# Adaptive-norm transformer block on one core: values in four sets a stage, a third slot of exponentials, and second halves' queries rotated by GpSimd

## The reference

```python
q = _rmsnorm(x @ wq_a.T, q_a_ln_w) @ wq_b.T           # per head 64 plain + 64 rotary columns
q_pe = _apply_rope(_deinterleave(q_pe), cos, sin)
scores = einsum('bqhd,bkhd->bhqk', q_full, k_full) * softmax_scale
scores = where(causal, scores, finfo.min)
attn = softmax(scores, axis=-1)
out = einsum('bhqk,bkhd->bqhd', attn, v)
out = out.reshape(B, S, H * VD) @ wo.T
```

## Time and profile before

| | us |
|---|---|
| median of 3 runs (721.63 to 721.87) | 721.75 |
| profiled execution, its own time | 721.88 |
| its span | 720.1 |
| TensorE busy | 694.4 (96%) |
| VectorE busy | 523.9 (73%) |
| ScalarE busy | 289.6 (40%) |
| GpSimd busy | 230.3 (32%) |

### The profile page before, as it was taken

The page is one execution under the profiler, slowest core; times in us unless marked ns, Lnnn a source line. Parts: engine busy times, 40 slices in busy tenths (PEclk is TensorE's granted clock), DMA queues, the critical chain, the costliest instruction groups (busy, mean ns, idle before and its releaser), DMA issues.

```text
span 720.1 us, 9320 instructions
## 1 busy us (share of the span) xinstructions
PE 694.4 (96%) x3539; PEld 478.6 (66%) x3539; DVE 523.9 (73%) x762; ACT 289.6 (40%) x427; POOL 230.3 (32%) x164
## 2 busy tenths in 40 slices
PE   2888899999999999999999999999999999999997
PEld 1864566666666666665665665556788888887886
DVE  6878799899899899899899886996882331323432
ACT  4752344544535444535444444452444222222120
POOL 2137641443453443443634402404651000000111
PEclk9999999999999999999999999999999999999999
DMA  8935542430430430331332833510211513100101
GB/s 317 279 89 133 134 108 58 108 74 15 107 88 1 107 88 20 88 88 33 74 89 44 292 134 116 179 59 3 87 29 32 143 46 88 47 1 1 44 30 44
DMA packets 40972, 63.34 MB, mean 88 GB/s; under 512 B 5536, under 2 KB 21664, under 8 KB 39072
## 3 DMA queue, kind: packets, MB, share of 16 engines
q1 hardware_dynamic: 40928, 62.75, 32.0%
HBM read 32.99 MB, written 2.10 MB: 49 GB/s over the span
## 4 chain that ended last, share of the span: by engine, by line
PE 88%; DVE 7%; ACT 2%; DMA 2%; issue 1%; SPq 1%; POOL 0%; DVEq 0%; ACTq 0%; POOLq 0%
PE PS L991 17%; PE PS L878 11%; PE PS L896 10%; PE PS L815 10%; PE PS L885 9%; PE PS L881 9%; PE PS L1008 8%; PE PS L955 5%; PE PS L801 4%; PE PS L827 2%; PE PS L835 1%; DVE MX L1433 1%; DMA PR<-in_wmod_c 1%; DVE PR L1328 1%; DMA Q<-TQ 1%
## 5 line engine op out<-in xcount | busy, mean ns | idle before, releaser
L1433 DVE TRANSPOSE_TENSOR_REDUCE MX<-PS 128x16 f32<-128x512 f32 x288 | 185.6, 689 | 36.4 <-PE PS L815 35.8
L1181 ACT ACTIVATE PR<-PS 128x1024 f32<-128x1024 f32 (+1 forms) x144 | 133.2, 931 | 186.6 <-PE PS L885 159.4
L878 PE MATMUL PS<-Q,KH 96*128 96x512 f32 x288 | 119.5, 415 | 0.1
L885 PE MATMUL PS<-Q,KH 97*128 97x512 f32 (+1 forms) x288 | 114.2, 396 | 0.3 <-DMA Q<-NM 0.3
L881 PE MATMUL PS<-Q,KL 96*128 96x512 f32 (+1 forms) x288 | 113.7, 395 | 0.0
L815 PE MATMUL PS<-Q,KH 96*128 96x512 f32 (+1 forms) x288 | 104.1, 424 | 1.8 <-DVE TQ L1423 1.2
L1528 DVE TENSOR_TENSOR PR<-PR 128x2048 f32<-128x2048 f32 (+1 forms) x40 | 92.2, 2305 | 0.8
L878 PEld LDWEIGHTS PS<-Q,KH 96*128 96x128 f32 x288 | 54.4, 189 | 49.8 <-issue 26.0
L815 PEld LDWEIGHTS PS<-Q,KH 96*128 96x128 f32 (+1 forms) x288 | 52.2, 189 | 35.2 <-issue 18.3
L896 PE MATMUL PS<-PR,V 128*32 128x512 f32 (+3 forms) x704 | 70.2, 486 | 0.0
L1655 DVE SCALAR_TENSOR_TENSOR wide<-PS,ffn_s,TQ 128x1024 f32<-128x1024 f32 x10 | 12.8, 1284 | 71.8 <-PE PS L991 71.8
(11 more groups left out here) (188 smaller groups left out, 1000.4 us busy)
## 6 DMA issues: line engine op xcount, KB each, us to landing
Q<-TQ SPq DMA_DIRECT2D x56, 384.0 KB, 6.5
RT<-in_wo SPq DMA_DIRECT2D x4, 1024.0 KB, 4.8
TQ<-in_wo SPq DMA_DIRECT2D x4, 1024.0 KB, 4.8
Q<-TQ SPq DMA_DIRECT2D x16, 192.0 KB, 3.4
WI<-in_gate_w SPq DMA_DIRECT2D x10, 256.0 KB, 3.3
WI<-in_up_w SPq DMA_DIRECT2D x10, 256.0 KB, 3.9
DI<-in_down_w SPq DMA_DIRECT2D x10, 256.0 KB, 2.7
PR<-in_wmod_c SPq DMA_DIRECT2D x2, 1024.0 KB, 6.5
```

The lines of the kernel that those rows point to most:

```text
L878: pe.matmul(dst, M.KH[0:KR, ks], M.Q[0:KR, w % 2, 0, qb, :, qs], start=True, stop=False)
L885: ins = pe.matmul(dst, M.KH[0:rows, ks], M.Q[0:rows, w % 2, 1, qb, :, qs], start=False, stop=True)
L1181: act.activation(tiles, banks, ACT.Exp).then_inc(S_.p, 1)
L1433: dve.tensor_reduce(M.MX[:, kt, qt // 4, :, qt % 4, :], PS[:, bank_of(turn), :].rearrange("p (h s q) -> p h s q", h=HG, q=L), axis=AX.X, o ...
```

## The change

Values and additions are no longer due by a lag; they are names in the table. In stages 0 to 6 values come in four sets: v0 to v3 with den1 of the stage before in unit 9, v4 and v5 in unit 19, v6 and v7 with den0 in unit 32, v8 to v11 in unit 0 of the next stage, with w behind them. Narrow steps share a slot with their neighbour, and there is a third slot, in the part of `attn` that groups 6 and 7 will fill (from stage 6 on in `TQ`). So x, which is read again into `TQ` for the residual, is loaded in the last stage, behind the fourth block of wo. The last stage uses the two old slots and has a table `LAST` with values and folds mostly together.

`HANDED` is now a rule by halves: group 1, and the second half (hf 1) of every later group. The tables also place the rotary work anew: even0 and odd0 in units 6 and 7, lat0 in 17, split0 in 22; even1 and odd1 in unit 29, lat1 in 34, split1 in 35.

```diff
-HANDED = (1,)
+def is_handed(g, hf):
+    return g == 1 or g > 1 and hf == 1
+
+HANDED = [(g, hf) for g in range(G) for hf in range(2) if is_handed(g, hf)]
...
+SHARED = [(s, s + 1) if units_of(s) == 2 else (s,) for s in ADDS if units_of(s) > 1]
+SLOTS = 3
+
+def slot_uses():
+    uses, last, turn = {}, {}, 0
+    for w in range(G):
+        for steps in SHARED if w < G - 1 else [(s,) for s in ADDS]:
+            slot = turn % SLOTS if w < G - 1 else steps[0] % 2
+            turn += 1
+            column = 0
+            for s in steps:
+                uses[w, s] = (slot, column, last.get(slot))
+                column += width(s)
+            last[slot] = (w, steps[-1])
+    return uses
...
 STAGE = [
-    "p w p", "", "p p",
-    "p p", "p", "p p even0 odd0",
...
+    "norm1 p p p", "", "p p", "p p", "join even1 odd1 a6", "", "rows a7", "v6,7 den0 inv0 norm0", "a8", "lat1 low1",
+    "a9 split1",
 ]
+LAST = [
+    "", "-a10", "-v8,9,10,11 fold0", "-a11", "", "", "v0 den1 inv1 fold1 norm1", "", "a1", "v1 fold2", "a2 gate0",
...
-            sp.dma_start(M.x1, t["x"].rearrange("(n p) d -> p n d", p=P)).then_inc(S_.xr, 16)
             sp.dma_start(M.WVF[:], t["wv"]).then_inc(S_.wv, 16)
...
     for m in range(2, G):
         load_wo(m)
+        if m == 3:
+            third = max((w, s) for w, s in USES if USES[w, s][0] == 2)
+            sp.wait_ge(S_.pv, NSTEP * third[0] + third[1] + 1)
+            sp.wait_ge(S_.ad, NADD * third[0] + ADDS.index(third[1]) + 1)
+            sp.dma_start(M.x1, t["x"].rearrange("(n p) d -> p n d", p=P)).then_inc(S_.xr, 16)
...
-        elif i == 0:
-            j = ADDS.index(s)
-            before = NSTEP * w + ADDS[j - 2] - (NSTEP if j < 2 else 0)
-            if before > 0:
-                act.wait_ge(S_.pv, before + 1)
-                act.wait_ge(S_.ad, NADD * w + j - 1)
+        elif i == 0 and USES[w, s][2] is not None:
+            before, step = USES[w, s][2]
+            act.wait_ge(S_.pv, NSTEP * before + step + 1)
+            act.wait_ge(S_.ad, NADD * before + ADDS.index(step) + 1)
...
-        elif kind == "odd" and g in HANDED:
+        elif kind == "odd" and is_handed(g, key[2]):
             rotate_odd(g, key[2])
+            if g > 1:
+                rotated_sum(g, key[2])
```

More of the change, by code:

```diff
@@ L115 @@
 NUNIT = len(UNITS)
[L116 to L133, removed]
+LATE_VALUES = LATE_SUMS = (NSTEP - 2, NSTEP - 1)
 WIDE_ADDS = [s for s in ADDS if not add_is_narrow(s)]
 NARROW_ADDS = [s for s in ADDS if add_is_narrow(s)]
+SHARED = [(s, s + 1) if units_of(s) == 2 else (s,) for s in ADDS if units_of(s) > 1]
[12 more added lines that the diff above has]
+    return uses
+USES = slot_uses()
 def blocks_of(qb):
@@ L378 @@
 STAGE = [
-    "p w p", "", "p p",
-    "p p", "p", "p p even0 odd0",
[L381 to L390, removed]
[4 rows of a table added]
+]
+LAST = [
[3 rows of a table added]
 ]
@@ L427, in group_places @@
 def group_places(g, places):
-    return [(place, (name[0], g) + name[1:], 0.0 if name[0] in ("even", "odd") and g in HANDED else busy)
+    return [(place, (name[0], g) + name[1:], busy)
             for place, name, busy in places]
[L433 to L470, removed]
+TABLES = [stage_table(w) for w in range(G)]
 FIRST_FOLDS = [("w", 0)]
@@ L937, in pe_program @@
             scores(w, s, i)
-            for ago, before in VALUES[n]:
-                if ago <= w:
-                    values(w - ago, before)
             for name in TABLES[w][n]:
-                side(name)
+                if name[0] == "values":
+                    for before in name[2]:
+                        values(name[1], before)
+                else:
+                    side(name)
     def product_term(st, n):
@@ L1216, in act_program @@
                 exponentials(w, e)
-            for ago, before in VALUES[n]:
-                if ago <= w and before in (3, NSTEP - 1):
-                    empty(w - ago, STEPS[before][0])
             for name in TABLES[w][n]:
-                side(name)
+                if name[0] == "values":
+                    for before in name[2]:
+                        if before in (3, NSTEP - 1):
+                            empty(name[1], STEPS[before][0])
+                else:
+                    side(name)
     empty(G - 1, 1)
@@ L1493, in side @@
         kind, g = key[0:2]
-        if kind == "even" and g not in HANDED:
+        if kind == "even" and not is_handed(g, key[2]):
             even(g, key[2])
-        elif kind == "odd" and g not in HANDED:
+        elif kind == "odd" and not is_handed(g, key[2]):
             odd(g, key[2])
@@ L1574, in dve_program @@
         for n in range(NUNIT):
[L1575 to L1577 removed]
             for name in TABLES[w][n]:
[L1579 removed]
+                if name[0] == "add" and name[2] in WIDE_ADDS:
+                    add(name[1], name[2])
+                else:
+                    side(name)
     for s in LATE_SUMS:
```

77 lines of the change are left out of this document (48 added, 29 removed), and 4 rows, old and new, of tables (LAST, STAGE).

## The result

The changed kernel takes 754.17 us in the median of 4 runs (753.23 to 755.96), the kernel before 721.81 beside it (721.63 to 721.87): a ratio of 1.0448, with a 95% interval of 1.0436 to 1.0461. Slower was forecast, but 733.6 us (717 to 742): the direction held, the size was 20.6 us short. The profiled execution took 755.96 us.

The account below looks back on a forecast made before the run. It took TensorE, busy for the whole 51.36 us of a middle stage, as the bound. From 721.88 us it took off 16.0 for fewer value runs and w, and added 27.7 of waits: 733.6 us, range 717 to 742.

Parts of the forecast that it names:

- the gain: TensorE in attention: 44 fewer runs of values at 0.34 us and 1.0 us on w save 16.0 us.
- the chain: From even1's matmuls at unit 29, ScalarE's copy, GpSimd's six operations taking turns with VectorE, split1, w's copies: 18.5 us.
- In all 5 x 4.8 + 3.7 = 27.7 us: TensorE's waits at stage starts: 4.8 us in each of stages 1 to 5, 3.7 in stage 6.
- the x load: Last stage, x loaded ahead of wo's fifth block: a delay of 0 to 3 us, taken as 0.
- hidden rotation: GpSimd's six second-half operations take under 11.5 us, so TensorE never waits: 706 us, chance 0.12.
- VectorE late: Turns with GpSimd delay VectorE's four additions, parts come late, 6 to 8 us of gain lost: 713 us, chance 0.08.
- gain and wait cancelling: A chain 2.0 us shorter leaves 16 us of TensorE waits, equal to the gain: 722 us, chance 0.08.

Follow-up runs that it names:

- short rotation: The changed kernel with GpSimd's six rotary operations for second halves of groups 2 to 7 cut to 64 of 512 columns: 715.04 us, ratio 0.9901.
- x late: The changed kernel with the load of x moved from behind the fourth block of wo to behind the eighth: 751.28 us.
- filled waits: The changed kernel with 16 matmuls of 128x512 added ahead of the fourth unit's scores in each of stages 1 to 6: 744.41 us.
- other places: The changed kernel with even1, odd1 at units 19, 21, other steps moved, x behind wo's last block: 715.73 us with the hand-over, 728.21 without.
- short additions: The changed kernel with VectorE's additions a6 to a9 of stages 0 to 6 cut to an eighth of their columns: 711.28 us, ratio 0.9857.

## Why the prediction missed

**Right: the gain, up to stage 6.** Stages without waits last 49.10 us, 49.1 in the prediction. By the transposition of the maxima in stage 6 (432.18 us before, 418.66 with the short rotation) 13.5 us are gained, 15.3 were due there: stage 0 gave 1.2 instead of 2.0, and stage 6 has a wait of 1.3 for queries. The last stage gave nothing of its 0.7: from there to the first product behind attention it is 52.3 us before and 52.8 with x late.

**Right: the chain.** Six operations in 15.3 us, four of them behind an addition, split1 held, then w's bank, then exponentials, at the starts of stages 1 to 6. The sum of TensorE's idle time there is 22.5 us (3.25 and 0.31 or 0.79 five times, 0.64 and 2.57 in stage 6), against 27.7.

**The step that failed:** "In all 5 x 4.8 + 3.7 = 27.7 us". It priced each wait at its own length. The short rotation shows the whole price: 754.17 - 715.04 = 39.1 us by the medians. Between the profiled executions it is 42.6 us up to the transposition in stage 6, in the changed kernel and with the short rotation:

```profile
461.30 0.30 PE L811 MATMUL PS<-ident,NMj 128*128 128x128 f32 x1 [0.77 <-DVE NMj L1441]
```

```profile
418.66 0.30 PE L811 MATMUL PS<-ident,NMj 128*128 128x128 f32 x1 [0.77 <-DVE NMj L1441]
```

Idle are 22.5 of it, and six small waits of 0.2 at unit 33; the wait for queries in stage 6 is 0.8 shorter than with the short rotation (0.46 against 1.28). That leaves 16 us by the medians and some 20 by the profiled executions, and the slow clock behind the waits is most of it: TensorE's busy time in the two stages shown is 3.5 and 3.0 us above 49.10 for the same matmuls. The filled waits show that the idle time is its cause. The stages of before could not show it: the clock was 1.00 there, for TensorE never stood. Only the start of that trace has a sign of it. After 12.24 us in which TensorE stands, four transpositions take 1.09 us, which take 0.60 later:

```profile
12.24 1.09 PE L741 MATMUL PS<-ident,x_in 128*128 128x128 f32 x4 [12.24 <-ACT x_in L1065]
...
21.71 0.60 PE L741 MATMUL PS<-ident,x_in 128*128 128x128 f32 x4
```

The clock's column reads 1.00 at both places, so that the first four had half the clock is a reading and not shown. The Trainium skill does say it (TensorE: Matmul & The Clock Gate, Part 1: The HAM clock gate (the "warmup" mystery)): the slow clock is the state of an idle array, and activity lifts it. The changed kernel's trace agrees with its 0.50 behind 3.2 us of idleness; by that rule the prediction should have carried a term for each wait.

**A second term, taken as 0:** the x load, 0 to 3 us in the working. It costs 2.9 to 4.7: 2.66 us at fold4, and the clock behind it, 0.62 from 496 to 500 us. From x's issue at 479.45 to fold4 at 494.35 are 14.9 us, as much as x's 10.1 and a block's 4.8 one behind the other: the upper end of the working held, and not the 0.

Together, by the positions in the profiled executions: 13.5 us gained and 42.6 lost up to stage 6's transposition, and 5.0 lost from there to the end (292.9 us against 287.9), most of them x. 721.88 - 13.5 + 42.6 + 5.0 = 756.0 us, and this execution took 755.96. Of the 42.6, some 3 us stand neither in the idle time nor in the clock's column; they were not located.

**The rivals.** The first, hidden rotation at 706 us, is what other places come near to with the same hand-over: its condition, six operations in under 11.5 us, holds there with 8.9, though the place also leaves ten us until split1. The second, VectorE late, comes when the hand-over is undone, by another way than the prediction's: not GpSimd's turns but VectorE's own four multiplications make its addition late. The third, gain and wait cancelling at 722, fell with the waits' price.

## What to carry to other kernels

A wait on an engine whose clock falls when it stands costs more than its length: here 3.5 to 4 us of idleness cost 6 to 7. Two engines that take turns can be half idle and still be the bound if their long instructions meet; ask not whether a moved step fits an engine's load, but what it meets at its new place and what stands behind the one that waits for it. Work that relieves a full engine may be needed and still stand in the wrong place: the hand-over gained 12.5 us at one place and lost 21 at another (754.17 with it, 732.78 without).

## What the runs showed of the hardware

Whether the clock falls is not set by a wait's length alone. Behind 3.2 us it fell in each of the five starts of stages 1 to 5. At fold4 it fell behind 2.56 us (short rotation) but not behind 2.31 (short additions). With the hand-over undone it fell behind one wait of 1.54 us, and not behind five others of 1.52 to 1.55. The two stretches behind fold4's wait, short rotation first:

```profile
453.00:457.00 4.00, 4.00 (x12) 2.82 (x9) 2.76 (x5) 1.02 (x1) 0.00 (x0) 0.50 0.59 199
```

```profile
452.00:456.00 4.00, 4.00 (x27) 2.04 (x25) 3.72 (x5) 2.05 (x2) 0.00 (x0) 1.00 0.71 262
```

And in the kernel with other places and no hand-over, about the same small waits (0.68 and 0.67 us, with TensorE busy for 1.09 and 1.21 of 2 us) left the clock whole in one stage and halved it in the next:

```profile
275.00:277.00 2.00, 1.09 (x4) 0.46 (x3) 2.00 (x5) 0.00 (x0) 0.00 (x0) 1.00 0.93 188
277.00:279.00 2.00, 2.00 (x9) 1.65 (x10) 2.00 (x4) 0.85 (x1) 1.99 (x2) 1.00 0.91 238
327.00:329.00 2.00, 1.21 (x4) 0.60 (x4) 2.00 (x4) 0.00 (x0) 0.37 (x1) 1.00 0.91 189
329.00:331.00 2.00, 2.00 (x8) 1.59 (x7) 1.90 (x4) 1.02 (x1) 2.00 (x2) 0.66 0.92 236
331.00:333.00 2.00, 2.00 (x6) 1.51 (x6) 0.00 (x0) 0.27 (x1) 1.38 (x2) 0.50 0.58 133
```

The kernel with the hand-over undone also spread more from run to run: 728.88 to 734.88 us, where the kernel before beside it took 721.64 to 723.58.
